# Attention sides counted as one run of units, projections three units behind their divisions, row shifts issued by ScalarE

## What is computed

```python
s = jnp.einsum('bhqd,bhkd->bhqk', q, k) / np.float32(np.sqrt(HD))
if mask is not None:
    s = jnp.where(mask, s, jnp.float32(-1000000000.0))
return jnp.einsum('bhqk,bhkd->bhqd', jax.nn.softmax(s, -1), v)
...
o1 = _attn(q, k1, v1, causal[None, None])        # all 1024 keys, causal
o2 = _attn(q, ks, vs)                            # 256 selected keys
o3 = _attn(q, kw, vw, winmask[None, None])       # a window of 64 keys
...
o = g[:, 0] * o1 + g[:, 1] * o2 + g[:, 2] * o3
o = o.transpose(0, 2, 1, 3).reshape(B, T, N_HEAD * VDIM)
return o @ Wproj
```

## Time and profile before

| | us |
|---|---|
| median of three runs | 2942.0 |
| lowest and highest | 2940.13, 2942.74 |
| the profiled execution | 2938.53 |
| its span in the trace | 2936.4 |

### The profile page before, as it was taken

The page is one execution under the profiler, slowest core; times in us unless marked ns, Lnnn a source line. Parts: engine busy times, 40 slices in busy tenths (PEclk is TensorE's granted clock), DMA queues, the critical chain, the costliest instruction groups (busy, mean ns, idle before and its releaser), DMA issues. The chain is left out here.

```text
span 2936.4 us, 47406 instructions
## 1 busy us (share of the span) xinstructions
PE 2361.4 (80%) x16660; PEld 1563.1 (53%) x16660; DVE 1690.2 (58%) x3159; ACT 1219.0 (42%) x2665; POOL 536.5 (18%) x575
## 2 busy tenths in 40 slices
PE   5666766665499999799999799999899999630896
PEld 3444535443365666465666465666465665320785
DVE  4754847466455664555665555665555665450676
ACT  2323423233054554354554355455355455410442
POOL 0230504215000110100110100110100110136332
PEclk9777877877699999899999899999899999855997
DMA  2361715427846556446556446556546643241113
GB/s 91 139 243 36 288 58 211 170 89 293 183 102 131 122 125 128 106 102 136 122 119 126 106 104 137 127 109 126 115 104 131 132 104 73 91 84 48 48 51 109
DMA packets 222999, 361.11 MB, mean 123 GB/s; under 512 B 68810, under 2 KB 124717, under 8 KB 222384
## 3 DMA queue, kind: packets, MB, share of 16 engines
q1 hardware_dynamic: 218448, 349.72, 47.7%
q0 software_dynamic: 4320, 8.43, 0.9%
HBM read 230.10 MB, written 126.56 MB: 121 GB/s over the span
## 5 line engine op out<-in xcount | busy, mean ns | idle before, releaser
L1342 ACT ACTIVATE prob<-ps 128x512 f32<-128x512 f32 (+5 forms) x1600 | 637.5, 441 | 740.8 <-PE ps L1293 587.5
L1395 DVE TENSOR_REDUCE maxima<-ps 128x1 f32<-128x512 f32 (+3 forms) x768 | 387.1, 547 | 299.2 <-PE ps L1224 151.2
L1314 PE MATMUL ps<-prob,plain 128*32 128x512 f32 (+5 forms) x3200 | 512.1, 443 | 0.0
L1400 DVE TENSOR_REDUCE maxima<-ps 128x2 f32<-128x512 f32 (+1 forms) x512 | 294.5, 607 | 245.0 <-PE ps L1232 98.6
L1365 POOL TENSOR_TENSOR products<-products,sums 128x256 f32<-128x256 f32 x192 | 140.7, 733 | 1611.3 <-DVE sums L1386 1610.1
L1386 DVE RECIPROCAL sums<-sums 128x256 f32<-128x256 f32 x192 | 331.5, 1736 | 104.2 <-ACT sums L1353 104.2
L1285 PE MATMUL ps<-q1a_s,k1a_s 128*128 128x512 f32 (+3 forms) x768 | 303.1, 395 | 0.0
L1293 PE MATMUL ps<-q1b_s,k1b_s 128*128 128x512 f32 (+3 forms) x768 | 301.1, 393 | 0.0
L1314 PE MATMUL ps<-prob,v_s 128*32 128x512 f32 (+3 forms) x1536 | 284.3, 491 | 0.0
L1221 PE MATMUL ps<-k1a_s,q1a_s 128*128 128x512 f32 (+3 forms) x768 | 233.3, 372 | 8.7 <-DMA k1a_s<-k1ah_dram 8.3
L1285 PEld LDWEIGHTS ps<-q1a_s,k1a_s 128*128 128x128 f32 x768 | 147.1, 192 | 126.8 <-issue 118.1
(11 more groups left out here) (329 smaller groups left out, 4774.3 us busy)
## 6 DMA issues: line engine op xcount, KB each, us to landing
qh_dram<-pairs SPq DMA_DIRECT2D x96, 512.0 KB, 3.7
kwh_dram<-pairs SPq DMA_DIRECT2D x64, 512.0 KB, 2.7
qa_s<-qh_dram SPq DMA_DIRECT2D x128, 256.0 KB, 4.5
kwa_s<-kwh_dram SPq DMA_DIRECT2D x128, 256.0 KB, 7.6
q1a_s<-qh_dram SPq DMA_DIRECT2D x128, 256.0 KB, 4.7
qb_s<-qh_dram SPq DMA_DIRECT2D x64, 256.0 KB, 9.2
kwb_s<-kwh_dram SPq DMA_DIRECT2D x64, 256.0 KB, 10.0
k1a_s<-k1ah_dram SPq DMA_DIRECT2D x32, 512.0 KB, 6.8
```

The source lines that it names most:

```text
L1314: mm = pe.matmul(ps[at:at + VD, SCORES + k % 2, q0 - c * CH:q0 - c * CH + w], w_, m.prob[:, n % PROBS, h, 0:w], start=first, stop=True, sk ...
L1342: act.activation(m.prob[:, u % PROBS, h, 0:w], ps[:, turn % SCORES, 0:w], ACT.Exp, scale=SCALE).then_inc(s["exp_done"], 1)
L1395: ins = dve.tensor_reduce(partial[:, h, i, part:part + 1], bank[:, 0:w], AX, ALU.max)
L1400: ins = dve.tensor_reduce(negs[1 if kind == "max1" else 2][:, at:at + 2], bank.rearrange("p (i n) -> p i n", i=2)[:, :, 0:w], AX, ALU.max, ...
```

## The change

The sides of a block are no longer planned one by one. Units are counted through the block from 0 to 199, and products are paired by this number. An odd side begins with an odd number, so there the pairs shift by one unit, and one pair holds unit 24 of an even side and unit 0 of the next. The single product at the end of a side is gone. `whole` and `rows` of branch 0 leave the end of the side: they stand behind unit 2 (`ROWS_AT`) of the next side, behind the `max2` fill there and ahead of the products. `proj` stands three units (`APART`) further behind its divisions. The row shifts are issued by ACT in the plan's order, which first waits until DVE has copied the row.

```diff
+ROWS_AT, APART = 2, 3
...
-    return todo + [("whole", side, 0)]
...
+    for n in range(total + 1):
+        w, u = divmod(n, len(UNITS))
...
+            if u == ROWS_AT and w > 0:
+                steps += [("whole", w, 0), ("rows", w, 0)]
+        ready = range(n - 2, n) if n >= 2 and n % 2 == 0 else ()
+        for done in ready:
+            steps.append(("products",) + divmod(done, len(UNITS)))
...
+                if w % 2 == 1:
+                    later += [("divide", w, k, piece) for piece in range(PIECES)]
+                    if SUMS[k][0] == 0:
+                        later += APART * [None] + [("proj", w, SUMS[k][1])]
+        steps += [x for x in later[:1] if x]
+        later = later[1:]
...
-                for br in (2, 1, 0):
-                    row(side, br)
...
+                if kind == "rows":
+                    br = step[2]
+                    dst, at = m.q1b if br == 0 else m.qb, ROWS[br]
+                    act.wait_ge(s["emptied"], plan.fills.index(step) + 1)
+                    act.dma_start(dst[at:at + 1, side % 2].rearrange("p h n -> p (h n)").bitcast(F32), m.mrows[:, br, :])\
+                        .then_inc(s["rows%d" % br], 16)
```

More of the change, by code:

```diff
@@ L946, in preparation @@
     todo = max2 + max1[:3] + [("rows", side, 2)] + max1[3:] + max0[:3] + [("rows", side, 1)] + max0[3:]
-    return todo + [("whole", side, 0)]
[L950 to L989, removed]
+    return todo
 class Plan:
@@ L1021, in block_plan @@
     sides = [k for k in range(1, NSIDE + 1) if k < NSIDE or not last]
[L1022 to L1026, removed]
+    total, columns = NSIDE * len(UNITS), sum(x[4] for x in UNITS)
+    steps, later = [], []
+    for n in range(total + 1):
+        w, u = divmod(n, len(UNITS))
+        if u == 0:
+            prepare, seen, at = preparation(w + 1) if w + 1 in sides else [], 0, 0
+        if n < total:
+            steps.append(("scores", w, u))
+            seen += UNITS[u][4]
+            upto = len(prepare) * seen // columns
+            steps += prepare[at:upto]
+            at = upto
+            if u == ROWS_AT and w > 0:
[3 more added lines that the diff above has]
+            steps.append(("products",) + divmod(done, len(UNITS)))
+        for done in ready:
+            w, u = divmod(done, len(UNITS))
+            if u in LAST:
+                k = LAST.index(u)
+                steps.append(("sum", w, k))
+                if w % 2 == 1:
[4 more added lines that the diff above has]
+        later = later[1:]
+    steps += [x for x in later if x]
+    if NSIDE in sides:
+        steps += [("whole", NSIDE, 0), ("rows", NSIDE, 0)]
     loads = [x for w in range(NSIDE) for x in (("whole", w + 1), ("local", w + 2)) if x[1] < NSIDE or not last]
     return Plan(steps, sides, loads)
-OPENING = Plan(preparation(NSIDE) + [("rows", NSIDE, 0)], [NSIDE],
+OPENING = Plan(preparation(NSIDE) + [("whole", NSIDE, 0), ("rows", NSIDE, 0)], [NSIDE],
                [("local", NSIDE), ("whole", NSIDE), ("local", NSIDE + 1)])
@@ L1165, in whole @@
                 sp.dma_start(m.v1[:, k].rearrange("p t n -> p (t n)"), src.v1).then_inc(late, 16)
[L1167 to L1173, removed]
             if cur is not None:
```

## The result

The changed kernel takes 3047.89 us (median of 4 runs, 3041.83 to 3056.40); the kernel before took 2941.52 us beside it. The ratio is 1.0364, with a 95% interval from 1.0337 to 1.0391: 3.6% slower, 106 us. The forecast was 3023 us, in a range from 2970 to 3065. The profiled execution of the changed kernel took 3050.75 us, with a span of 3048.6.

A forecast was written before the change was run, and what follows sets the result against it. PE was taken to set the pace in attention sides, so its waits count. On the median of 2942 us, -24 + 58 + 51 + 0 - 4 = +81 gave 3023 us, range 2970 to 3065.

The forecast's parts named there:

- Removed waits, 24 us: PE's waits ahead of projections and side-end transposes, plus the single product's starts, go: 6.1 us a block, 24 in four.
- Moved transpose, 58 us: Behind S2, PE waits 1.0 us on odd sides and 3.5 on even ones: 14.5 us a block, 58 in four.
- Reciprocals against fills, 51 us: On odd sides, shifted pairs bring six reciprocals one unit later against fills: net 3.2 us a side, 51 us in all.
- The four places: Odd-side fills behind S7, S13, S15 and S19, where PE waits for emptied banks: 4.0 us together.
- About 55: Length forecast for even sides, in us; odd sides were to take 56 to 57.
- ACT's row shifts, 0: 96 issues of 0.50 us on ACT cost nothing, being covered; 48 us if the cover were gone.
- Block ends, -4 us: At a block's end SP stores t2a without the row shift ahead: about -1 us a block, -4 us.
- rival B: The clock falls in PE's 12 waits: 16 to 54 us more, 3039 to 3077 us; chance 0.15.
- A: Only the moved transpose costs; fills on odd sides find their banks free: 2972 us; chance 0.17.
- C: Faster: the waits vanish and none takes their place, `whole` being done before the transpose: 2918 us; chance 0.07.
- D: Gains and losses cancel, or the order matters less than listed: within 0.2%; chance 0.04.
- two signs of being wrong: Even sides staying under 53.5 us, or PE waiting for exponentials held up by ACT's row shifts.

The follow-up runs named there:

- The last run with SP as issuer: The both causes undone kernel, with the last group's divisions of odd sides one unit later and row shifts issued by SP: 2927.19 us, ratio 0.9961.
- short reciprocals: The changed kernel with each DVE reciprocal of the attention on 64 of 256 columns, the other three quarters left out: 2942.09 us, ratio 1.0009.
- `whole` early: The changed kernel with DVE's `whole` moved to the head of the side, ahead of the max2 reduces and both reciprocals: 2999.36 us, ratio 1.0206.
- pairs within the side: The changed kernel with products paired within each side as before, 22, 23 and 24 together at the side's end: 2977.91 us, ratio 1.0137.
- both causes undone: The changed kernel with `whole` at the head of the side and products paired within each side: 2943.35 us, ratio 1.0014.

## Why the forecast held, and where it was off

- **What bounds the kernel.** Right. PE set the pace, and the time moved with its waits. DVE, busy for 58% of the span, was free only on average.
- **Removed waits, 24 us.** This term is mis-sized by some 12 us. The waits at projections did go, but alone that is worth 11.5 us, for which the forecast had 16: on even sides 0.5 us and not 0.9. The other 8 us, for the transpose's 0.2 us at a side's end and for the single product, did not come. The last run with SP as issuer has the transpose behind unit 2 with no wait of PE ahead of it inside a block, and is level with the later projections alone (2927.19 and 2928.46 us). And a pair of sides takes 106.9 us in the changed order with short reciprocals, which is the 104.8 of the later projections alone plus two waits of 1.0 at transposes: the single product's share is not to be seen.
- **Moved transpose, 58 us.** Right. The replay put the transpose at 9.5 us, it came at 9.56; it had 2.7 us of wait and 2.50 were measured, 0.8 at the fill ahead of it, where the scores-to-fill distance grew by 0.7. On odd sides 1.0 was forecast, 0.8 measured as idle and 1.0 as distance (2.18 us from S2 to S3 against 1.19 with `whole` early). Moving `whole` alone gave back 48.5 us, of which 11 are the falls of the clock.
- **Reciprocals against fills, 51 us.** The four places were the right ones, and their net is about right, but by two errors that cancel, which is luck. On side 3 of the third block the steps at these places are 0.6, 0.7, 0.8 and 1.2 us longer than with short reciprocals; forecast were 0.65, 1.3, 1.0 and 1.05. That is 3.3 us and not 4.0. The 0.8 us less waiting for exponentials did not come: PE waited for them for 18.2 us in all and 20.5 before. Net 3.3 against 3.2 a side. The whole effect of the pairing is larger than this term, since its later sum is also in the 3.5 us at the head of even sides: undoing it was worth 70 us, with part of the clock in it.
- **Even sides.** "About 55" was forecast and 56.4 measured with the clock up. Half of that, 0.7 us, is product work that the shifted pairs move over from odd sides, which the sign left out and which costs nothing over the pair; the other half is the removed wait that was over-sized.
- **ACT's row shifts, 0.** Right for the changed kernel (SP in its place: no difference). The bound of 48 us never came near; about 12 us were measured where nothing else covered the wait.
- **Block ends, -4 us.** About right. The transpose there stands 1.2 us further behind the projection (4.7 us for 3.5), and the next block starts 1.6 to 2.1 us sooner after it: 0.4 to 0.9 us less a block.
- **The clock.** The forecast's own sum put it at nothing. It was rival B, with a chance of 0.15. At the seven waits the clock stood at 1.2 GHz for 31 us in all, for 11 us of time: 0.36 us for each. The forecast had read 0.45 from block starts; the 18.0 and 21.7 us there are the first 128 matmuls of a block and not its first side, as the forecast has it. The run with the transpose moved alone gives 0.42 (20 us for 48). The Trainium skill ("TensorE: Matmul & The Clock Gate", Part 1) has it that activity releases the throttle; the run with two matmuls in the wait agrees, with no fall in 12.
- **The sum.** Of the 25 us between 3023 and 3048, some 12 are the over-sized removed waits and 11 the clock; the other terms were off by 1 to 3 us each, so it does not close to the microsecond. The measured time lies in rival B's band (3039 to 3077), but B does not account for it alone: its least price was 16 us, and the falls gave 11. The range held because it was stretched upwards for the clock, while half of the gap has another cause.
- **Rivals A, C, D.** The fills did not find their banks free, the wait at the transpose did not vanish, and gains and losses did not cancel. Of the two signs of being wrong, neither came: even sides are over 53.5 us, and PE's waits for exponentials did not grow.

## What to carry to other kernels

An engine that is half idle on average can still be the one that its neighbour waits for, if it works in order and holds instructions of 1.7 us among ones of 0.5: before a step is moved, count what stands ahead of it on every engine it needs, not only on the one that waits. A tuned order is a set of small slacks (0.45 us here), so changing the parity of pairs or the place of one reduce should be replayed against the trace place by place; and parts of a change should be timed apart, since here the one good part, 0.3% faster alone, was lost under two bad ones.

## What the hardware showed

- The same standstill of PE, 2.50 us long and always in the same place of the program, was followed by a fall of the granted clock at 7 of 12 places in the changed kernel, at 9 of 12 with SP as issuer and at 11 of 12 with the transpose moved alone. Waits of 0.5 and 1.2 us, 5.4 us apart (the run with `whole` early), had none in 12. But waits of 0.3, 0.7 and 0.9 us, the first and the last 4.1 us apart, with scores and fills between, had 5 in 12 (the run with pairs within the side), and two of 0.4 and 0.7 us without the third had none (both causes undone). What decides between a fall and none at the same place stays open.
- A row shift of 8 KB landed 1.8 us (least) to 2.7 us (median) after its issue from ACT in the changed kernel; its issue took 0.51 us there, and for branch 0 0.50 on SP in the kernel before.
